# The second product of a two-sided adjacency kernel in rounds of 4, 6, 8, 8 and 14 row tiles in place of 10, 14 and 16

## What is computed

```python
u = par_u[0] * par_u[1] * (diag_u[:, None] * x[:2048] @ W_u) + x[:2048]
i = par_i[0] * par_i[1] * (diag_i[:, None] * x[2048:] @ W_i) + x[2048:]
e = concat([u, i])                       # 5120 x 64
h = adj @ (adj.T @ e)                    # adj is 5120 x 5120, f32
y = layernorm(h) * gamma + beta + x
x1 = layernorm(x + y)
out = layernorm(x1 + hypergraph_layers(x1, adj))
```

## Time and profile before

| | |
|---|---|
| median of 3 runs | 415.06 us |
| the profiled execution | 414.27 us |
| its span | 412.5 us |
| around the span | 1.77 us |
| TensorE (matmuls) busy | 383.8 us, 93% |
| VectorE busy | 324.7 us, 79% |
| ScalarE busy | 266.6 us, 65% |
| GpSimd busy | 68.6 us, 17% |
| HBM read | 107.6 MB |

### The profile page before, as it was taken

One profiled execution on the slowest core, in us unless ns is written; L12 is line 12 of the kernel. 1 busy time (PEld: TensorE's weight loads), 2 busy tenths in 40 slices (PEclk: granted clock), 3 DMA queues, 4 the chain that ended last, 5 costly groups with the idle time before them and its releaser, 6 DMA issues.

```text
span 412.5 us, 13885 instructions
## 1 busy us (share of the span) xinstructions
PE 383.8 (93%) x6018; PEld 223.2 (54%) x6018; DVE 324.7 (79%) x404; ACT 266.6 (65%) x497; POOL 68.6 (17%) x122
## 2 busy tenths in 40 slices
PE   8987999999999999999999999999999999999940
PEld 7543555565464455546445554644555464668740
DVE  3699769799695979769786966988696697694783
ACT  3696938799888488578848857884785688100220
POOL 2001100303003000300200030011003001169663
PEclk9999999999999999999999999999999999999995
DMA  8999999954992998399389929957992995400002
GB/s 293 386 387 381 386 386 387 382 217 144 388 386 109 322 387 314 114 388 385 138 289 379 354 83 373 387 184 260 385 370 55 392 386 202 130 4 3 29 27 82
DMA packets 56706, 109.87 MB, mean 266 GB/s; under 512 B 3776, under 2 KB 3904, under 8 KB 56640
## 3 DMA queue, kind: packets, MB, share of 16 engines
q1 hardware_dynamic: 56352, 108.84, 72.6%
q10 hardware_dynamic: 288, 0.09, 0.1%
HBM read 107.60 MB, written 1.31 MB: 264 GB/s over the span
## 4 chain that ended last, share of the span: by engine, by line
PE 51%; DMA 23%; SPq 18%; DVE 2%; issue 2%; POOL 1%; ACT 0%; DVEq 0%; ACTq 0%
PE pair L1382 39%; DMA pooled<-in_adj 22%; SPq L977 17%; PE pair L1363 10%; PE pair L1395 2%; DMA pooled<-in_x 2%; POOL pooled L1052 1%; DVE pooled L1204 1%; SPq L968 1%; DVE pooled L1182 1%; SPq L963 1%; POOL pooled L1047 0%; DVE pooled L1272 0%; DVE pooled L1264 0%; DVE pooled L1293 0%
## 5 line engine op out<-in xcount | busy, mean ns | idle before, releaser
L1086 ACT ACTIVATE scratch<-pooled 128x1024 bf16<-128x1024 f32 x200 | 210.5, 1053 | 63.8 <-DMA pooled<-in_adj 61.9
L1182 DVE STREAM_TRANSPOSE pooled<-pooled 128x1024 f32<-128x1024 f32 x200 | 228.8, 1208 | 11.3 <-ACT scratch L1086 8.9
L1363 PE MATMUL pair<-pooled,rows_in 128*64 128x256 f32 x1600 | 186.0, 383 | 10.7 <-DMA pooled<-in_adj 10.3
L1382 PE MATMUL pair<-pooled,col_sum 32*64 32x320 f32 (+3 forms) x4224 | 177.4, 485 | 0.9 <-DVE pooled L1204 0.5
L1363 PEld LDWEIGHTS pair<-pooled,rows_in 128*64 128x64 f32 x1600 | 109.6, 137 | 88.4 <-DMA pooled<-in_adj 31.1
L1382 PEld LDWEIGHTS pair<-pooled,col_sum 32*64 32x64 f32 x4224 | 94.0, 132 | 78.7 <-issue 57.0
L1204 DVE TENSOR_TENSOR pooled<-pooled,pair 128x320 f32<-128x320 f32 (+3 forms) x120 | 58.1, 545 | 44.6 <-PE pair L1382 44.6
L1022 POOL COPY col_sum<-col_half 32x256 f32<-32x256 f32 x80 | 31.6, 394 | 317.6 <-DVE col_half L1191 314.6
L1095 ACT COPY col_sum<-col_half 32x256 f32<-32x256 f32 x80 | 32.2, 403 | 11.1 <-DVE col_half L1191 10.3
L1086 ACT ACTIVATION_READ_ACCUMULATOR scratch<-pooled 128x1 f32 x200 | 37.4, 187 | 0.0
L1113 ACT ACTIVATE pooled<-pair 128x512 f32<-128x512 f32 x5 | 3.0, 598 | 39.3 <-PE pair L1395 39.3
(11 more groups left out here) (47 smaller groups left out, 62.2 us busy)
## 6 DMA issues: line engine op xcount, KB each, us to landing
pooled<-in_adj SPq DMA_DIRECT2D x200, 512.0 KB, 10.1
pooled<-in_x SPq DMA_DIRECT2D x5, 256.0 KB, 3.7
out<-pooled SPq DMA_DIRECT2D x5, 256.0 KB, 2.0
pooled<-in_x SPq DMA_DIRECT2D x1, 768.0 KB, 6.9
pooled<-in_x SPq DMA_DIRECT2D x1, 512.0 KB, 3.7
pooled<-in_w_ui ACTq DMA_DIRECT2D x1, 64.0 KB, 2.9
beta_sb<-in_beta SPq DMA_DIRECT2D x1, 32.0 KB, 9.0
pooled<-in_scales ACTq DMA_DIRECT2D x1, 22.0 KB, 3.2
```

The source lines that it names most:

```text
L1086: nc.scalar.activation(scratch[v % 2][:, :], slots[slot_of(v)], ACT.Square, accum_out=square_sum[:, v:v + 1]).then_inc(unit_scanned, 1)
L1182: nc.vector.transpose(tiles, tiles).then_inc(unit_turned, 1)
L1363: mm = pe.matmul(block_bank[c % 2][half(h), 0:w // 2], rows_in[:, t, :], slots[slot_of(v)][:, at:at + w // 2], start=(t == 0), stop=(t == ...
L1382: mm = pe.matmul(round_banks(g)[a][half(b % 2), 0:w].rearrange("p (t r) -> p t r", r=32), col_sum[c % 2][quadrant(a), b, :], to[quadrant(a ...
```

## The change

`PARTS` gives blocks 1 to 7 five rounds of 4, 6, 8, 8 and 14 row tiles, and block 8 four of 6, 10, 10 and 14. Blocks 0 and 9 keep theirs. VectorE's order takes up the new rounds: after `turn_half` one unit, then additions and the other units in turn. The row sums of x are taken in the head, in five parts, from the first load of x; `x_sum` gets a tile of its own, SyncE waits for the sums before it lets block 1's units overwrite x, and GpSimd now waits for the second load of x itself and centers all five groups before the first `root_c`. `turn_half(0)` comes four units before the end of block 0 in place of two.

```diff
--- before
+++ after
@@ -44,8 +44,9 @@
     SLOT_FIRST = [20 if c % 2 == 0 else 0 for c in range(NB)]
     assert sum(WIDTHS) == N and max(WIDTHS) == CH
 
-    PARTS = [((0, 10), (10, 14), (24, 16))] * (NB - 2)
-    PARTS += [tuple((t, 10) for t in range(0, T, 10)), tuple((t, 8) for t in range(0, T, 8))]
+    PARTS = [((0, 10), (10, 14), (24, 16))]
+    PARTS += [((0, 4), (4, 6), (10, 8), (18, 8), (26, 14))] * (NB - 3)
+    PARTS += [((0, 6), (6, 10), (16, 10), (26, 14)), tuple((t, 8) for t in range(0, T, 8))]
     ROUNDS_AT = [sum(len(parts) for parts in PARTS[:c]) for c in range(NB + 1)]
     LAST = ROUNDS_AT[NB - 1]
     NR = ROUNDS_AT[NB]
@@ -111,9 +112,9 @@
         X_SLOT = 20
         x_at = SLOT * X_SLOT
         x_all = pooled[:, x_at:x_at + T * D].rearrange("p (t d) -> p t d", d=D)
-        x_sum, c_sum, var, rstd, y_sum, y_var, y_eps, x1_rstd, scale = (
-            pooled[:, x_at + T * D + T * i:x_at + T * D + T * i + T] for i in range(9))
-        ln_at = x_at + T * D + 9 * T
+        c_sum, var, rstd, y_sum, y_var, y_eps, x1_rstd, scale = (
+            pooled[:, x_at + T * D + T * i:x_at + T * D + T * i + T] for i in range(8))
+        ln_at = x_at + T * D + 8 * T
 
         def ln_buffer(i):
             a = ln_at + GT * D * i
@@ -135,6 +136,7 @@
         center_t = sb("center_t", [D, P])
         center_g = sb("center_g", [D, D])
         beta_sb = sb("beta_sb", [P, D])
+        x_sum = sb("x_sum", [P, T])
         beta_sum = sb("beta_sum", [P, 1])
         square_sum = sb("square_sum", [P, UNITS])
         part_max = sb("part_max", [P, 1])
@@ -970,6 +972,7 @@
 
                     assert SLOT_FIRST[1] == 0 and SETUP_SLOTS <= UPB[1]
                     sp.wait_ge(e_made, LGROUPS)
+                    sp.wait_ge(x_summed, LGROUPS)
                 before = before_in_slot(v)
                 if before:
                     b, ib = place_of_unit(before[-1])
@@ -1028,9 +1031,10 @@
 
 
             pool.wait_ge(cols_kept_pool, NB)
-            pool.wait_ge(x_summed, 1)
+            pool.wait_ge(x_summed, LGROUPS)
             nc.gpsimd.tensor_scalar(x_sum[:, :], x_sum[:, :], 1.0 / D, None, ALU.mult).then_inc(x_steps, 1)
             pool.wait_ge(beta_steps, 3)
+            pool.wait_ge(x_again, 16 * 2)
 
             def center_x(k):
                 xk = x_all[:, group_tiles(k), :]
@@ -1052,12 +1056,10 @@
                 nc.gpsimd.tensor_tensor(scale[:, group_tiles(k)], y_var[:, group_tiles(k)], minus_half[:, :],
                                         ALU.pow).then_inc(scale_made, 1)
 
-            for k in range(LGROUPS - 1):
+            for k in range(LGROUPS):
                 center_x(k)
+            pool.wait_ge(x_steps, 1 + 3 * LGROUPS)
             root_c(0)
-            pool.wait_ge(rstd_made, 1)
-            center_x(LGROUPS - 1)
-            pool.wait_ge(x_steps, 1 + 3 * LGROUPS)
             root_c(1)
             root_y(0)
             root_c(2)
@@ -1140,6 +1142,13 @@
         @block.vector
         def _(dve):
             nc.vector.memset(h_sum[:, 0:WARM], 0.0).then_inc(warm_cleared, 1)
+
+            def sum_x(k):
+                dve.wait_ge(x_loaded[k], 16)
+                nc.vector.tensor_reduce(x_sum[:, group_tiles(k)], x_first[:, group_tiles(k), :], X,
+                                        ALU.add).then_inc(x_summed, 1)
+
+            sum_x(0)
             dve.wait_ge(scales_in, 16)
             nc.vector.tensor_tensor(pp[:, :], par_sb[:, 0:4:2], par_sb[:, 1:4:2], ALU.mult).then_inc(diag_made, 1)
             dve.wait_ge(diag_made, 1)
@@ -1204,19 +1213,22 @@
                         added = nc.vector.tensor_tensor(to, to, share, ALU.add)
                 added.then_inc(round_added, 1)
 
+            sum_x(1)
             make_e(0)
             make_e(1)
             make_e(2)
+            for k in range(2, LGROUPS):
+                sum_x(k)
             for v in range(3):
                 turn_unit(v)
             make_e(3)
             for v in range(3, 7):
                 turn_unit(v)
             make_e(4)
-            for v in range(7, UPB[0] - 2):
+            for v in range(7, UPB[0] - 4):
                 turn_unit(v)
             turn_half(0)
-            for v in range(UPB[0] - 2, UPB[0]):
+            for v in range(UPB[0] - 4, UPB[0]):
                 turn_unit(v)
 
 
@@ -1235,24 +1247,30 @@
                 for v in range(first, first + 13):
                     turn_unit(v)
                 turn_half(c + 1)
-                for v in range(first + 13, first + 15):
-                    turn_unit(v)
-                add_round(ROUNDS_AT[c])
-                if c < NB - 2:
-                    for v in range(first + 15, UNIT_FIRST[c + 2]):
-                        turn_unit(v)
+                turn_unit(first + 13)
+                if c == NB - 2:
+                    turn_unit(first + 14)
+                    add_round(ROUNDS_AT[c])
+                    turn_unit(first + 15)
+                    turn_unit(first + 16)
                     add_round(ROUNDS_AT[c] + 1)
+                    turn_unit(first + 17)
+                    turn_unit(first + 18)
                     add_round(ROUNDS_AT[c] + 2)
+                    turn_unit(first + 19)
+                    add_round(ROUNDS_AT[c] + 3)
                 else:
-                    for v in range(first + 15, first + 17):
-                        turn_unit(v)
+                    add_round(ROUNDS_AT[c])
+                    turn_unit(first + 14)
                     add_round(ROUNDS_AT[c] + 1)
-                    dve.wait_ge(x_again, 16 * 2)
-                    nc.vector.tensor_reduce(x_sum[:, :], x_all[:, :, :], X, ALU.add).then_inc(x_summed, 1)
+                    turn_unit(first + 15)
+                    turn_unit(first + 16)
                     add_round(ROUNDS_AT[c] + 2)
-                    for v in range(first + 17, UNITS):
-                        turn_unit(v)
+                    turn_unit(first + 17)
+                    turn_unit(first + 18)
                     add_round(ROUNDS_AT[c] + 3)
+                    turn_unit(first + 19)
+                    add_round(ROUNDS_AT[c] + 4)
             dve.wait_ge(unit_scanned, UNITS)
             nc.vector.tensor_reduce(part_max[:, :], square_sum[:, :], X, ALU.max).then_inc(max_found, 1)
             add_round(LAST)
```

## The result

The changed kernel takes 451.54 us (median of 4 runs, 450.9 to 453.73), against 414.73 us for the kernel before (4 runs). The ratio is 1.0905 (95% interval 1.0856 to 1.0953). Forecast were 403.0 us and a range of 401 to 409. The profiled execution is the one of 453.73 us and has a span of 451.9 us. In what follows, the medians of runs 2, 3, 7 and 10 include one execution that was slower at a lower clock; the ratios leave it out.

A forecast was written before the change was run, and what follows sets the result against it. TensorE's waits for adj units, through a transfer loop including the first round, were taken as the bound. From 414.27 us, -12.2 + 0.6 - 0.5 = -12.1 gave 402.2, or 403.0 us as a median; range 401 to 409 us.

The forecast's parts named there:

- What bounds the kernel: Blocks 1 to 7: TensorE's own period is 34.79 us, the measured 36.53 us because it waits for late adj units.
- the loop of transfers: First round frees slots for the next block's adj loads; its length is in the 36.53 us period, falling to 34.0 us.
- Rival E: Transfers do not start earlier, nothing comes of the change, period stays at 36.5 us: 414 to 415 us; chance 4%.
- Six waits a block in seven blocks: Reading of TensorE's 42 waits for adj units, 10.3 us in total, as a pattern over blocks 1 to 7.
- The rate of short matmuls: TensorE's short rounds: 128 columns take 1.75 us by the rate of long rounds; 1.8 us was taken.
- Rival B: Short rounds lose to weights (2.0 to 2.2 us a round) or falling issue rate: 404.5 to 409 us; chance 18%.
- Rival C: Issue floor, 24 ns a matmul or more, makes short rounds slower than before: about 420 us; chance 9%.
- The step that failed: TensorE's period in blocks 1 to 7 becomes 34.87 us, above the transfers' 34.0 us, so TensorE sets it.
- two open costs: TensorE in short rounds: issue, one matmul and its weights each 13.3 ns, and weight loading, 0.12 to 0.14 us per 128 columns.
- upper bound of a short round: TensorE's 128-column first round was bounded between 1.75 and 3.45 us.
- VectorE: Additions grow from 6.15 to 6.71 us a block, hidden in idle time; no round waits, except +0.6 us once in the first period.
- Row sums of x: Sums moved to the head cost zero there; VectorE's lateness at block 8 goes, -0.5 us.

The follow-up runs named there:

- run 2: Kernel before with the change's rounds and order of additions, row sums of x taken late as before: 446.19 us, ratio 1.0744.
- run 3: Kernel before with its own rounds, but matmuls of rounds in blocks 1 to 7 cut along columns to 320 a block: 444.94 us, ratio 1.0725.
- run 7: Kernel before with four rounds of 6, 8, 12 and 14 row tiles in blocks 1 to 7: 440.94 us, ratio 1.0643.
- run 10: Kernel before with rounds placed between the next block's units and the change's five rounds in blocks 1 to 7: 451.54 us, ratio 1.0894.
- run 5: Kernel before without the adj loads of blocks 2 to 9, output not the reference's: 403.79 us, ratio 0.9762.
- run 8: Kernel before with each block's first round moved ahead of the next block's last three units, same matmuls: 409.36 us, ratio 0.9887.
- run 12: Kernel before with rounds of 10, 14 and 16 between units in blocks 1 to 7 only, x sums in the head: 405.32 us, ratio 0.9802.
- run 1: The change without its rounds: rounds and addition order of before, x sums in the head, new centering order: 413.01 us against 413.53, ratio 0.9978.
- run 4: Kernel before with rounds of 8, 16 and 16 row tiles in blocks 1 to 7, no more matmuls: 420.35 us, ratio 1.0165.

## Why the prediction was wrong

- **What bounds the kernel: right.** TensorE's own period of 34.79 us was measured by run 5 to the hundredth, and that the loop of transfers goes through the first round is shown by runs 8 and 12, which gain by breaking it. Rival E did not come. One reading on the way was wrong: "Six waits a block in seven blocks" counts 42 waits, of which 15 lie ahead of block 1's first round; the seven blocks have 27 (6.1 us), about four each. The sum did not use it.
- **The forecast of 34.0 us for the transfers' loop: not tested.** In the changed kernel the scans of one block's units go from 143.77 to 174.12 us, 30.35 us in place of 26.45, but its rounds, which free the slots, were late themselves.
- **The rate of short matmuls: nearly right.** "A round of 128 columns is then 1.75 us", and 1.8 was taken: 128 records of 128 columns started within 1.89 us, 15 ns each, and the first 224 records of a block within 3.86 us. Rival B is refuted in its first form, weights at 2.0 to 2.2 us a round. Rival C is refuted as it was put, an issue floor of 24 ns or more, and with it here the rule of 25 ns from start to start that the prediction quoted from the Trainium skill, "TensorE: Matmul & The Clock Gate", section "Wait — 56ns, not 53.3ns?". Its sign was right, by another mechanism.
- **The step that failed** is "TensorE. Its period becomes 17.42 + 17.37 + 2 x 0.04 = 34.87 us if short rounds run at the rate of long ones", and its two open costs. It asked at what rate the array takes matmuls and weights and at what rate a full queue issues them. It never asked at what rate instructions come into the core. It went from a burst of 8 matmuls in 70 ns to a rate for 320. Supply was the cost, with the lower clock that its stalls brought: 7.5 us a block, 42.4 in place of 34.9.
- **A hint of it was there.** The page before listed 49 packets of 0.80 MB in an instruction queue, 16 KB each. The fastest round that any row showed was 128 records in 3.88 us, and the change asks for 1.75. What a packet takes under traffic, no row of before said. The prediction set 3.45 us as an upper bound of a short round, the time of a 256-column one. With a new cause beyond every row, that was no bound.
- **VectorE: right.** In the steady part it waits 0.5 us for the product's end before it turns the half, and no round waits for it. Only in the first period does TensorE wait for the half, 0.38 us by the timeline's idle time, forecast as 0.6.
- **Row sums of x: open.** Forecast -0.5 us; the tail became 2.2 us shorter in the changed kernel (451.9 - 390.32 = 61.6 against 63.75), 2.6 us in run 1. But in run 1 all that stands ahead of the tail took 2.4 us longer, and the run as a whole is 0.5 us faster with an interval that reaches 1. So a gain in the tail is seen, and one in the time is not shown.
- **The range** held no case of a loss: case C was the only mechanism for one, at 9%, and its price (420 us) was too low besides.

## What to carry to other kernels

Cutting a stage into finer pieces multiplies instructions; on TensorE compare the time that 128 matmuls (256 instructions with their weight loads) take in the densest few microseconds with the 4 to 7 us that the next 16 KB of instructions took here. Stalls put down to issue, 127 or 128 matmuls apart or a multiple of that, are its mark. Where a wait for a transfer closes a loop through one short stage, move that stage earlier in the order before cutting it smaller.

## What the runs showed of the hardware

- TensorE's instructions came in packets of 16 KB. Under traffic of adj 3.9 to 6.9 us passed between the ends of two stalls one packet apart, and the denser matmuls cost 37 us; without that traffic the same program lost some 2.2 us a block.
- A packet took 0.9 to 1.5 us with traffic or without, and TensorE went on 1.2 to 1.6 us after its end. What grew with traffic is the time until it started, from 1.1 to 3.7 us in the median.
- Matmuls on eight pieces of the array started 15 to 17 ns apart over 128 to 224 of them.
- Beside stalls of 2.2 to 2.7 us the granted clock fell to its lower level for a part of a block, in four of the seven windows.
- A queue of transfers ran dry for a microsecond, and the next three units landed 2.6, 2.6 and 2.3 us apart, not 1.39 (run 4). Whether the gap is the cause is open.

Open is what a packet of instructions waits for before it starts, and whether transfers that leave room would shorten it. This was not tried.
